# All sixteen experts' first weights held on chip in a ViT block with a mixture of experts, and split from there by a register address

## The reference, cut to what matters

```python
h = tok(x)                                   # 28x28 patches of 128 images -> 64 tokens + class token, D = 128
h = h + sigmoid(concat(window_attention(ln(h)), ln(h)) @ W_c)
z = ln(h)
# expert layer: E = 16, DH = 4*D = 512, TOP_K = 2
g    = layer_norm(z, ln_in_g, ln_in_b)
gate = softmax((g @ router_w + router_b) / 0.7)
vals, idx = top_k(gate, 2)
eh   = silu(einsum('bsd,edh->ebsh', g, ew1) + eb1)      # ew1: E x 128 x 512, the "first weights"
ey   = einsum('ebsh,ehd->ebsd', eh, ew2) + eb2          # ew2: E x 512 x 128, the "second weights"
moe  = sum over the two chosen experts of vals * ey
     + 0.25 * (silu(g @ sw1 + sb1) @ sw2 + sb2)         # shared expert
ff   = silu(layer_norm(moe, ff_ln_g, ff_ln_b) @ ff_w1 + ff_b1) @ ff_w2 + ff_b2
out  = h + (z + moe + ff)
```

## Time and profile before

| | us |
|---|---|
| median of 3 runs | 904.56 (903.32 to 905.45) |
| the profiled execution, time | 902.83 |
| the profiled execution, span | 901.0 |

### The profile page before, as it was taken

One profiled execution on the slowest core, in us unless ns is written; L12 is line 12 of the kernel. 1 busy time (PEld: TensorE's weight loads), 2 busy tenths in 40 slices (PEclk: granted clock), 3 DMA queues, 4 the chain that ended last, 5 costly groups with the idle time before them and its releaser, 6 DMA issues. The chain is left out here.

```text
span 901.0 us, 21734 instructions
## 1 busy us (share of the span) xinstructions
PE 863.4 (96%) x5920; PEld 787.8 (87%) x5920; DVE 677.3 (75%) x2244; ACT 595.7 (66%) x1064; POOL 441.3 (49%) x374
## 2 busy tenths in 40 slices
PE   2999999999999999999988999999999999799998
PEld 1778888888888888888877999999999999699888
DVE  8468877788788777887785777777776775788784
ACT  2566767776666767776874666666666665587776
POOL 7012345555654545555462665655555666234441
PEclk9999999999999999999998999999999999899999
DMA  9999999999999999949437788888887874334432
GB/s 223 224 219 233 234 239 240 233 235 235 237 241 244 246 253 245 242 126 288 147 101 204 241 255 246 248 252 247 249 254 236 242 236 127 103 100 121 106 94 54
DMA packets 194305, 187.01 MB, mean 208 GB/s; under 512 B 16797, under 2 KB 168698, under 8 KB 194010
## 3 DMA queue, kind: packets, MB, share of 16 engines
q1 hardware_dynamic: 183168, 166.24, 69.9%
q0 software_dynamic: 9376, 19.42, 7.0%
q10 hardware_dynamic: 1722, 0.93, 0.4%
HBM read 150.48 MB, written 36.04 MB: 207 GB/s over the span
## 5 line engine op out<-in xcount | busy, mean ns | idle before, releaser
L1450 PE MATMUL bank<-xf,wp 128*128 128x256 f32 x1280 | 309.4, 390 | 5.5 <-ACT xf L642 5.4
L1450 PEld LDWEIGHTS bank<-xf,wp 128*128 128x128 f32 x1280 | 234.6, 189 | 47.7 <-issue 4.3
L927 POOL DMA_INDIRECT y_tok<-region,dsti x160 | 164.4, 1027 | 125.1 <-DVE region L1283 95.6
L885 POOL TENSOR_TENSOR rstd<-var,neghalf 128x4 f32<-128x4 f32 (+2 forms) x51 | 80.2, 1573 | 262.8 <-DVE var L1041 133.8
L642 ACT ACTIVATE xf<-region 128x1024 f32<-128x1024 f32 x160 | 174.1, 1136 | 21.0 <-DVE region L958 21.0
L901 POOL DMA_INDIRECT z_rows<-z,posg x130 | 158.8, 1221 | 43.3 <-issue 42.7
L1654 PE MATMUL bank<-region 128*128 128x128 f32 x1280 | 155.8, 275 | 0.0
L1654 PEld LDWEIGHTS bank<-region 128*128 128x128 f32 x1280 | 149.9, 192 | 0.0
L809 ACT ACTIVATE region<-bank,cols 128x256 f32<-128x256 f32 x320 | 126.3, 476 | 21.7 <-PE bank L1643 21.1
L958 DVE COPY region<-region 32x1792 f32<-32x1792 f32 x96 | 106.1, 1105 | 41.2 <-ACT hT L662 22.0
L1643 PE MATMUL bank<-parts 128*128 128x256 f32 x960 | 136.1, 292 | 0.2
(11 more groups left out here) (183 smaller groups left out, 1210.5 us busy)
## 6 DMA issues: line engine op xcount, KB each, us to landing
region<-in_x SPq DMA_DIRECT2D x384, 196.0 KB
region<-in_L_ffn_ew SPq DMA_DIRECT2D x160, 256.0 KB
region<-z_rows SPq DMA_DIRECT2D x80, 130.0 KB
region<-y_tok SPq DMA_DIRECT2D x16, 512.0 KB, 3.5
ht_dram<-hT SPq DMA_DIRECT2D x16, 256.0 KB, 8.0
r_dram<-rr SPq DMA_DIRECT2D x16, 256.0 KB, 7.6
region<-ht_dram SPq DMA_DIRECT2D x16, 256.0 KB, 5.8
region<-r_dram SPq DMA_DIRECT2D x16, 256.0 KB
```

What stands on the lines that cost most here:

```text
L885: pool.tensor_tensor(dst, var, neghalf[:, 0:var.shape[1]], ALU.pow).then_inc(ready, 1)
L927: pool.indirect_dma_start(y_tok, bass.IndirectOffsetOnAxis(dsti[n % 2][:, i:i + 1], 0), yout[n % 2][:, i], None).then_inc(y_free[n % 2], 16)
L1450: ins = pe.matmul(out_cols, wp[:, s], cols_in, start=s == 0, stop=s == MAIN - 1)
```

## The change

All 16 first weights get a place of their own on chip, `w1all`, 16 x 512 columns, and each is loaded once. Eight of them (`W1_LOW` = 8) fit into the first half of `region` behind the shared buffers, which is free of images earlier; they are loaded at the end of stage one, four before the stores of group 12 and four after the `ht` blocks. The other eight lie in the second half and are loaded after the rows of tiles 0 to 3. `first_weight` goes. `split_w1` reads the expert's number of its tile from `ejc` with a function `expert` (a plain number for tiles below 16, a load into a register otherwise; in the loop it is always the load) and takes its source from `w1all` at that address. `rows_out` uses the same function, so the first four tiles make no such load any more. In place of a wait for each load DVE waits for the four first ones, for the group of low ones and for the group of high ones, each once. `xf`, `xlast` and `wp` move into a longer `region`, whose columns are reused for the biases, `shs`, `zin` and `yout`; the weights of stage three get arrays of their own. In SP's queue the second weights of the first four tiles move behind the wait for the last image copies, and the six later `ht` blocks ahead of it. Rows and second weights are loaded per tile as before.

```diff
@@ buffers
-        w1b = [carve(W) for _ in range(4)]
+        r_res = carve(TILES * D)
+        w1_at = carved[0]
+        w1all = carve(E * W)
+        W1_LOW = (XCOLS - w1_at) // W
...
@@ SP, end of stage one
-            for i in range(HT_LOW):
+            def load_w1(e, done):
+
+                sp.dma_start(w1all[:, e * W:(e + 1) * W], ew1[e]).then_inc(done, 16)
+
+            for i in range(FIRST_HT):
                 load_ht(i)
-            for j in range(FIRST):
-                sp.dma_start(w1b[j], ew1[j]).then_inc(w1_loaded[j], 16)
-                sp.dma_start(w2b[j], ew2[j].rearrange("(c p) d -> p c d", p=P)).then_inc(w2_loaded[j], 16)
+            for e in range(FIRST):
+                load_w1(e, w1_loaded[e])
             one(stores, GROUPS - 3)
...
+            for i in range(FIRST_HT, EARLY):
+                load_ht(i)
+            for e in range(FIRST, W1_LOW):
+                load_w1(e, w1_low)
+            one(stores, GROUPS - 2)
             sp.wait_ge(xact_ready, units_before(GROUPS, 0))
-            for i in range(HT_LOW, EARLY):
-                load_ht(i)
-            one(stores, GROUPS - 2)
+            for j in range(4):
+                sp.dma_start(w2b[j], ew2[j].rearrange("(c p) d -> p c d", p=P)).then_inc(w2_loaded[j], 16)
...
@@ SP, start and loop of the expert stage
-            first_weight(FIRST)
+            for e in range(W1_LOW, E):
+                load_w1(e, w1_high)
...
                 if j + 1 < EXPERT_TILES:
                     expert_rows(j + 1)
-                    first_weight(j + 1)
                 second_weight(j)
...
@@ DVE
-            def split_w1(j, n, h):
-
+            def expert(j):
+
+                return j if isinstance(j, int) and j < E else \
+                    dve.value_load(ejc[0:1, bass.ds(j, 1)], min_val=0, max_val=E - 1)
+
+            def split_w1(j, n):
+
+                ex = expert(j)
                 dve.wait_ge(up_done, j * EC - EC) if n > 1 else None
-                dve.wait_ge(w1_loaded[n % 4], h * 16 + 16)
-                dve.tensor_copy(w1h[n % 2], w1b[n % 4]).then_inc(w1h_ready, 1)
+                w1 = w1all[:, bass.ds(ex * W, W)]
+                dve.tensor_copy(w1h[n % 2], w1).then_inc(w1h_ready, 1)
                 dve.wait_ge(w1h_ready, j + 1)
-                dve.tensor_tensor(w1l[n % 2], w1b[n % 4], w1h[n % 2], ALU.subtract).then_inc(w1l_ready, 1)
+                dve.tensor_tensor(w1l[n % 2], w1, w1h[n % 2], ALU.subtract).then_inc(w1l_ready, 1)
...
-                ex = dve.value_load(ejc[0:1, bass.ds(j, 1)], min_val=0, max_val=E - 1)
+                ex = expert(j)
...
-            for j in range(4):
-                step2(j, j)
+            dve.wait_ge(w1_loaded[2], 16)
+            step2(0, 0)
+            dve.wait_ge(w1_loaded[3], 16)
+            step2(1, 1)
+            dve.wait_ge(w1_low, 16 * (W1_LOW - FIRST))
+            step2(2, 2)
+            step2(3, 3)
+            dve.wait_ge(w1_high, 16 * (E - W1_LOW))
             dve.wait_ge(w3_loaded, 48)
```

More of the change, by code:

```diff
@@ L69 @@
 FILL, EARLY = 7, 12
+FIRST_HT = 6
 SP_TAILS = 12
@@ L169, in carve @@
             carved[0] += n
[L170 removed]
+            assert carved[0] <= ARENA
             return region[:, carved[0] - n:carved[0]]
@@ L176, in build @@
         ht3 = [carve(GTOK) for _ in range(2)]
+        r_res = carve(TILES * D)
         assert carved[0] <= XCOLS
-        shared_with_stage3 = carved[0]
-        w1b = [carve(W) for _ in range(4)]
+        w1_at = carved[0]
+        w1all = carve(E * W)
+        W1_LOW = (XCOLS - w1_at) // W
         w2b = [carve(W).rearrange("p (c d) -> p c d", c=EC) for _ in range(4)]
-        eh_at = carved[0]
         ehT = [carve(EC * EROWS).rearrange("p (c r) -> p c r", c=EC) for _ in range(2)]
+        h2T = [carve(EROWS) for _ in range(2)]
+        assert carved[0] <= 2 * XCOLS
+        sh_res = carve(TILES * D)
+        assert carved[0] >= 2 * XCOLS
+        eb2_rows = carve(E * D)
+        shs = [carve(SC * GTOK).rearrange("p (c r) -> p c r", c=SC) for _ in range(2)]
         zin = [carve(EH * ZW).rearrange("p (h d) -> p h d", h=EH) for _ in range(4)]
-        h2T = [carve(EROWS) for _ in range(2)]
         yout = [carve(EH * D).rearrange("p (h d) -> p h d", h=EH) for _ in range(2)]
-        fw1_t = carve(DH)
-        fw2_t = carve(EC * D).rearrange("p (c d) -> p c d", c=EC)
-        r_at = carved[0]
-        r_res = carve(TILES * D)
-        HT_LOW = (XCOLS - r_at) // GTOK
-        sh_res = carve(TILES * D)
-        carved[0] = shared_with_stage3
+        fw1_t = sb("fw1_t", [P, DH])[:, :]
+        fw2_t = sb("fw2_t", [P, EC * D])[:, :].rearrange("p (c d) -> p c d", c=EC)
+        carved[0] = w1_at
         moe = [carve(GT * D).rearrange("p (t d) -> p t d", t=GT) for _ in range(2)]
@@ L207, in build @@
         h2h, h2l = ([parts[:, 4 * W + (2 * c + u) * EROWS:4 * W + (2 * c + u + 1) * EROWS] for u in range(2)] for c in range(2))
-        xf = sb("xf", [P, QUADS * 4 * HTOK])
+        xf = region[:, 2 * XCOLS:2 * XCOLS + XF]
         xquad = [xf[:, u * 4 * HTOK:(u + 1) * 4 * HTOK].rearrange("p (q t j) -> p q t j", q=2, j=2) for u in range(QUADS)]
-        xlast = sb("xlast", [P, HTOK])
-        eb2_rows = xf[:, 0:E * D]
-        shs = [xf[:, E * D + u * SC * GTOK:E * D + (u + 1) * SC * GTOK].rearrange("p (c r) -> p c r", c=SC) for u in range(2)]
+        xlast = region[:, 2 * XCOLS + XF:2 * XCOLS + XF + XL]
+        wp = region[:, 2 * XCOLS + XF + XL:ARENA].rearrange("p (s h) -> p s h", s=MAIN)
         wparts = sb("wparts", [P, 2 * DH + 2 * DS], F32R)
@@ L330, in build @@
         tail_ready, ejb_done, ejt_ready, tej_done = sem("tail_ready"), sem("ejb_done"), sem("ejt_ready"), sem("tej_done")
-        w1_loaded = [sem(f"w1_loaded{u}") for u in range(4)]
+        w1_loaded = [sem(f"w1_loaded{u}") for u in range(FIRST)]
+        w1_low, w1_high = sem("w1_low"), sem("w1_high")
         w2_loaded = [sem(f"w2_loaded{u}") for u in range(4)]
@@ L501, in _ @@
             zero_tails(sp, 0, FIRST)
-            experts = list(range(E))
-            def first_weight(j):
-                if j >= E:
-                    experts.append(sp.value_load(ejc[0:1, j:j + 1], min_val=0, max_val=E - 1))
-                sp.wait_ge(w1l_ready, j - 3)
-                sp.dma_start(w1b[j % 4], ew1[bass.ds(experts[j], 1)].rearrange("o d h -> d (o h)"))\
-                  .then_inc(w1_loaded[j % 4], 16)
             def second_weight(j):
+                ex = j if j < E else sp.value_load(ejc[0:1, j:j + 1], min_val=0, max_val=E - 1)
                 sp.wait_ge(down_done, j - 3)
-                sp.dma_start(w2b[j % 4], ew2[bass.ds(experts[j], 1)].rearrange("o (c p) d -> p (o c) d", p=P))\
+                sp.dma_start(w2b[j % 4], ew2[bass.ds(ex, 1)].rearrange("o (c p) d -> p (o c) d", p=P))\
                   .then_inc(w2_loaded[j % 4], 16)
@@ L1256, in _ @@
             ht_low(FILL + 3)
-            split_w1(0, 0, 0)
+            dve.wait_ge(w1_loaded[0], 16)
+            split_w1(0, 0)
             dve.wait_ge(tej_done, 1)
```

15 lines of the change are left out of this document (7 added, 8 removed).

## The result

| | before | changed |
|---|---|---|
| median of 20 runs each, us | 904.42 (901.41 to 907.90) | 906.51 (904.15 to 909.31) |
| the profiled execution: span, time | 901.0, 902.83 | 904.7, 906.53 |

The ratio is 1.0026, 95% interval 1.0016 to 1.0036: the changed kernel is slower by a quarter of a per cent, 2.1 us. That lies inside the range, but it isn't the likeliest case of the prediction, which was no change.

The account below looks back on a forecast made before the run. The prediction took PE (TensorE), without a gap in the expert stage, as the bound. Profiled 902.8 us plus 0 + 0 + 0 for three parts, plus 1.7 to the median, gave 904.6 us; range 902.6 to 909.0, forecast's own 903.0 to 906.2.

Parts of the forecast that it names:

- the likeliest case of the prediction: Whole kernel: no change within 0.2% (1.8 us), chance 0.60.
- Part 1: Expert stage: 80 first-weight loads become 16; PE waits for none of them, so 0 us.
- Nothing before 480 us is on a path of PE that I can find: 0 us: Before the expert stage: moved transfers delay no work of PE, 0 us.
- Part 2: SP's queue at expert stage start: seven more issues ahead of tile 4's rows, no stall, 0 us.
- the cover: Tile 4's rows: margin between landing and PE's transposes at 495.82, between 0 and 4 us.
- rival B: Expert stage start: tile 4's rows late, 2 us idle plus clock loss, 906.6 to 909.2 us; chance 0.08.
- Part 3: DVE's loop: new register load per tile makes four tiles 13.5 to 13.9 us against PE's 13.7; 0 us lost.
- The path: DVE's loop, h2 subtraction to w1h copy: 0.99 us with the uncovered register load, 0.37 before.
- the middle loses nothing: DVE's loop: the middle of its four-tile range, 13.7 us, costs PE 0 us.
- Rival A: Expert loop: DVE becomes the bound, 14.0 us per four tiles, 2.9 us lost, 907.5 us; chance 0.24.

Follow-up runs that it names:

- the first trace: Profiled execution of the changed kernel as first measured, against the kernel before: 906.53 us, span 904.7.
- the second: The changed kernel, unaltered, profiled and timed again: 907.1 us, ratio 1.0040 to the kernel before.
- the second load: Changed kernel with the register load in the first-weight split made twice for tiles from 16 on, second value unused: 940.37 us in one execution.
- the control: The kernel before, unaltered, profiled again: 905.08 us in one execution, span 903.2.
- the ring: Changed kernel with rows of tile 4 ahead of the high first weights and each expert number loaded once, kept in four registers: 907.14 us, ratio 1.0036.

## Why the prediction was partly right

**The transfers that go (Part 1): right.** PE stayed at 40.00 us busy of 40.00, the DMA share fell to 0.58 where "about 0.6" was forecast, and the scatter waits shrank without PE's matmuls coming earlier. The added load on the kernel before refines it: of the gain something reached DVE, and was spent there.

**"Nothing before 480 us is on a path of PE that I can find: 0 us": wrong, 0.9 us.** This is the one term of the loss that every trace repeats, and it had no place in the sum. The step looked at transfers and their order, but the diff also moved `wp`, an operand of PE's most frequent instruction, and I gave that edit neither a price nor a range. The rows of the kernel before could not have priced it; that it deserved a bound could be seen, since 1344 patch matmuls (16 groups of 84) make 1 ns each into more than 1 us.

**The queue (Part 2): the step failed that took the cover as enough.** The rows of tile 4 were to be issued at 489.2; the start of the stage aside (483.62 in place of 480.90), that would be 491.9, and it was 492.57. The rest is in the transfer. They were to land 11 to 13 us after the first row block was issued; they landed some 15 us after it in the first trace (483.62 to 498.61) and 15.3 in the second (484.71 to 500.05). That is what rival B had with 250 GB/s: 15.6 us, landing near 498. Both factors of the term were too kind: from 483.62 to 498.61 the changed kernel moved 290 GB/s (284 in 489 to 491), not 348 to 356, and that is 4.35 MB, not 3.9, since other transfers run beside those that were counted. The stall was 0.76 and 2.52 us, where B said 2, and the clock's fall came once. A chance of 0.08 was too little for something that one of two traces shows nearly in full and the other in part.

**DVE (Part 3): the mechanism right, the conclusion a bit short.** The path was forecast at 0.99 us and measured 0.92 to 0.93. The turn was to be 13.5 to 13.9 us and was 13.71. That the middle came out so well is in part luck, since single terms missed in both directions: the four load paths came 0.07 us shorter each, and in the fourth tile of a turn the step to the low half was 0.69 us instead of 0.46 and the step to dsti 1.16 instead of 0.82. I took "the middle loses nothing". It loses little by itself: 0.4 and 0.1 us in the two traces. What the step lacked is that an engine at the pace of the bound can't make up a disturbance, so that a late scatter near the start reaches PE, 0.4 us in one trace and 1.1 in another. Rival A's mechanism (DVE as the bound throughout the loop, 2.9 us) did not occur; 0.62 us a tile more and it does, as the second load showed.

By the figure of the Trainium skill (DMA: Bandwidth & Descriptors, Latency and other measured facts, a floor of about 600 ns for a tensor_load) the path was an estimated 0.87 us; the measured step lies between this and the forecast. In these traces the load instruction alone takes 0.31 us, under that floor, and only with its register operations 0.62. The same row speaks of unrolling by four to spread the cost; the load of seven values at once saved little, 0.55 us a value.

**Sum.** 0 + 0 + 0 was forecast; 0.9 + 1.0 + 0.4 came in the first trace and 0.9 + 4.3 + 0.1 in the second. The number landed inside the range, but not by the forecast's account: its largest repeated term was not in the range's working at all. The result is on the slower side, to which I had given 0.32, through the mechanism of B in part and not through that of A.

## What to carry to other kernels

- Where one engine is full and a transfer share is high, ask who waits for a transfer before taking traffic away. Here 16.8 MB less gave PE nothing, and the address that replaced them cost VectorE nearly all its slack.
- Bringing a second engine to the pace of the first is not free even if the sum says equal: after it a late transfer near the start of the loop reaches PE.
- A burst of large loads was in the way of small ones that were due soon, and moving the first victim ahead of it only found the next. Spreading the burst behind the small ones took PE's waits for rows away; the ratio went from 1.0036 to 1.0013, but the intervals overlap. And an edit that only moves an operand of the busiest instruction needs a range too.

## What was not expected of the hardware

- A number read from on-chip memory into a register of VectorE costs 0.62 us with its register operations where nothing covers it, half of it the load instruction (0.31 us). Seven values in one load take 1.70 us and with their register operations 3.84 us of idle time, 0.55 a value.
- With the token weights moved into the array of the images stage one takes 0.9 us more than 353.2, in ten traces with them moved and in none of four without. The time stands between matmuls that stream `xf` (1.3 ns a step) and not behind those that stream `xlast`; the cause is open.
- TensorE's clock does not follow the length of the last gap alone. At the start of this stage it fell to half after gaps of 1.87 to 3.21 us in thirteen traces and not after the one of 1.65 us at 486.92 (up matmuls of 1.70 us). But in front of it, at 462 to 468 us, behind gaps of 1.2 and 0.93 us that all fourteen traces have, it fell in five traces and not in nine: in the control, and not in the first trace of the same kernel.
- The same rows, issued in nearly the same place of the queue, took 6.0 us in one execution and 7.0 in the other to reach PE, and those of tile 5 with the ring 9.0 us (493.75 to 502.74).
